# Moving two DMA issues, one matmul group, one vector add and four filler matmuls inside a four-engine pipeline

## The reference

```python
# second block, for each of 32 batches: attention with hyperbolic distances, 16 heads of 8
diff_sq = q_norm_sq + k_norm_sq - 2.0 * qk
denom = (1.0 - c * q_norm_sq) * (1.0 - c * k_norm_sq)
denom = jnp.maximum(denom, 1e-06)
cosh_arg = jnp.maximum(1.0 + 2.0 * c * diff_sq / denom, 1.0)
dist = jnp.arccosh(cosh_arg)
attn = softmax(-dist);  x = x + (attn @ v) @ wo.T
# then an MLP with 512 hidden units
x = x + jnp.einsum('bsw,wd->bsd', relu(layernorm(x) @ w1 + b1), w2) + b2
```

## Time and profile before

| what | value |
|---|---|
| median of 3 runs | 2447.98 us (2444.44 to 2456.33) |
| profiled execution, its own time | 2456.33 us |
| span of its trace | 2454.2 us |
| mean granted TensorE clock | 0.907 of full speed |
| busy over the span: PE, DVE, ACT, POOL | 85%, 80%, 72%, 66% |
| second block, first to last | about 1330 us to the end |

### The profile page before, as it was taken

How to read it: one execution, slowest core, us unless ns; L and a number is a source line. 1 busy time by engine, 2 the same in 40 slices (tenths; PEclk the granted TensorE clock), 3 DMA queues, 4 the chain that set the end, 5 groups by cost and what they waited for, 6 DMA issues and landing times. The chain is left out here.

```text
span 2454.2 us, 50808 instructions
## 1 busy us (share of the span) xinstructions
PE 2089.9 (85%) x15438; PEld 1566.8 (64%) x15438; DVE 1956.8 (80%) x5939; ACT 1767.4 (72%) x3085; POOL 1627.2 (66%) x1866
## 2 busy tenths in 40 slices
PE   4999999999999996999997677777777778777876
PEld 4677777777777775888885445555555555555554
DVE  4677776776777774778775899999999999999992
ACT  2666666666666762444432799999999999999996
POOL 2776676766666750000001899999999999999993
PEclk7999999999999996999997579888888988889888
DMA  5000000000000003353450466776666777666674
GB/s 142 1 2 2 2 1 2 2 1 2 1 2 1 2 2 70 86 119 76 96 114 10 93 127 130 139 138 128 124 119 127 141 141 134 119 129 124 129 142 80
DMA packets 81388, 184.24 MB, mean 75 GB/s; under 512 B 9479, under 2 KB 31530, under 8 KB 81195
## 3 DMA queue, kind: packets, MB, share of 16 engines
q0 software_dynamic: 36864, 134.23, 29.1%
q1 hardware_dynamic: 36010, 43.38, 7.9%
q10 hardware_dynamic: 8320, 4.19, 0.7%
HBM read 42.85 MB, written 4.72 MB: 19 GB/s over the span
## 5 line engine op out<-in xcount | busy, mean ns | idle before, releaser
L1557 POOL TENSOR_TENSOR spare<-spare,u 128x1024 f32<-128x1024 f32 x192 | 456.2, 2376 | 16.0
L542 ACT ACTIVATE prob<-s_ps,nmax 128x128 f32<-128x128 f32 (+1 forms) x1024 | 364.4, 432 | 132.2 <-DVE nmax L599 132.2
L599 DVE CUSTOM_DVE_ANT_0 s_ps<-s_ps,mask 128x128 f32<-128x128 f32 (+1 forms) x1024 | 340.7, 385 | 100.7 <-issue 76.4
L1633 DVE TENSOR_SCALAR u<-d_ps 128x1024 f32<-128x1024 f32 x256 | 312.1, 1219 | 48.7 <-PE i_ps L1374 48.1
L579 POOL TENSOR_TENSOR g_lo<-g_all,g_hi 128x512 fp32r<-128x512 f32 x256 | 329.1, 1286 | 21.4
L1637 DVE SCALAR_TENSOR_TENSOR u<-i_ps,u 128x1024 f32<-128x1024 f32 x256 | 313.5, 1225 | 13.2 <-DVE u L1633 0.5
L1374 PE MATMUL d_ps<-rowsT 28*128 28x256 f32 x1024 | 144.7, 357 | 149.5 <-DVE u L1637 145.9
L534 ACT COPY g_all<-g_ps 128x512 f32<-128x512 f32 x256 | 151.5, 592 | 162.6 <-PE g_ps L63 161.5
L1514 ACT ACTIVATE u<-u 128x1024 f32<-128x1024 f32 x256 | 257.0, 1056 | 1.7 <-DMA u<-spare 1.6
L1517 ACT ACTIVATE u<-u 128x1024 f32<-128x1024 f32 x256 | 255.7, 1051 | 0.0
L1374 PEld LDWEIGHTS d_ps<-rowsT 28*128 28x128 f32 x1024 | 92.4, 208 | 246.3 <-issue 241.7
(11 more groups left out here) (275 smaller groups left out, 5795.2 us busy)
## 6 DMA issues: line engine op xcount, KB each, us to landing
u<-spare POOLq DMA_DIRECT2D x256, 512.0 KB, 12.2
w_all<-w_rows SPq DMA_DIRECT2D x128, 256.0 KB, 5.9
x<-L_attn_x ACTq DMA_DIRECT2D x8, 512.0 KB, 13.9
y<-x SPq DMA_DIRECT2D x32, 128.0 KB, 10.0
wkqv<-L_attn_Wkqv SPq DMA_DIRECT2D x4, 528.0 KB, 8.9
gate_rows<-L_ffn_gate_proj SPq DMA_DIRECT2D x1, 512.0 KB, 14.4
up_rows<-L_ffn_up_proj SPq DMA_DIRECT2D x1, 512.0 KB, 11.1
down_cols<-L_ffn_down_proj SPq DMA_DIRECT2D x1, 512.0 KB, 13.0
```

What stands on the lines that cost most here:

```text
L542: last = nc.scalar.activation(prob[:, kind, at, :].rearrange("p c n -> p (c n)"), s_ps[kind][:, at.start * P:at.stop * P], ACT.Exp, bias=n ...
L599: last = nc.vector.tensor_tensor_reduce(out=scores, in0=scores, in1=keep.mask[:, N - width:N], scale=-1.0, scalar=3.4e38, op0=ALU.add, op1 ...
L1557: nc.gpsimd.tensor_tensor(extra, extra, pair, ALU.mult).then_inc(prod_done, 1)
L1633: nc.vector.tensor_scalar(u[:, slot(i, p), :], d_ps[:, :], 0.0, None, ALU.max).then_inc(dist_done, 1)
```

## The change

Five edits, all in the written orders of the second block:

1. POOL issues sums 0 and 1 behind product 4, ahead of product 5; sums 2 to 7 stay behind product 5.
2. The first half of the hidden layer moves from the end of p = 1 to p = 2, ahead of `pe_values`, so both halves stand at one place in the loop.
3. Filler matmuls in a batch go from 6 to 10: one is new ahead of the values at p = 3, six instead of four stand behind p = 4, two instead of one behind p = 7.
4. On DVE `dve_y` at p = 1 stands ahead of the copies of rows 5 and 6 instead of behind them.
5. The wait for a late copy, used in the last batch alone, moves with edit 2.

```diff
-    SUMS_BEHIND = {5: (0, 1, 2, 3, 4, 5, 6, 7)}
+    SUMS_BEHIND = {4: (0, 1), 5: (2, 3, 4, 5, 6, 7)}
-    HIDDEN_AT = (1, 3)
-    BUSY_AHEAD, BUSY_BEHIND = {5: 1}, {4: 4, 7: 1}
+    HIDDEN_AT = (2, 3)
+    BUSY_AHEAD, BUSY_BEHIND = {3: 1, 5: 1}, {4: 6, 7: 2}
...
-                        if four_before and p == HIDDEN_AT[1]:
-                            pe_hidden(pe, b - 4, 1, (b + 1) * (HP // 2))
+                        if four_before and p in HIDDEN_AT:
+                            if not one_after:
+                                pe.wait_ge(late_xT4_done, 1)
+                            pe_hidden(pe, b - 4, HIDDEN_AT.index(p), (b + 1) * (HP // 2))
                         if one_before and p in VALUES_AT:
                             pe_keep_busy(BUSY_AHEAD.get(p, 0))
...
-                        if four_before and p == HIDDEN_AT[0]:
-                            if not one_after:
-                                pe.wait_ge(late_xT4_done, 1)
-                            pe_hidden(pe, b - 4, 0, (b + 1) * (HP // 2))
...
+                        if p == 1 and five_before:
+                            dve_y(dve, b - 5)
                         for r in {0: (4,), 1: (5, 6), 2: (7,)}.get(p, ()):
                             copy_rows(dve, b, r, i)
-                        if p == 1 and five_before:
-                            dve_y(dve, b - 5)
```

## The result

The changed kernel is slower: 2568.57 us median of 4 runs (2557.45 to 2572.67) against 2447.4 us for the kernel before (four runs here), ratio 1.0489 (95% interval 1.0448 to 1.0531). The sign was forecast, the size was not: +121 us where I had +56.

A forecast was written before the change was run, and what follows sets the result against it. A loop through four engines, loop B at 34.94 us, was to bind; with 0.4 for slow stretches, 35.3 against 33.3 us over 27 batches gave 54 us, plus 2 at the end: 2504 us median, range 2470 to 2540.

The forecast's parts named there:

- The step that failed: TensorE: filler at p = 3 and moved hidden half cost nothing; 0.4 and 1.0 us if the waits covering them go.
- loop B: From mark over POOL's norm, PE's MLP output, DVE's residual and copies to next mark: 34.94 us, expected to bind.
- Loop A: ACT and POOL alone: sums 0 and 1 delay root 5 from 6.70 to 8.5 us; 33.87 us; rival chance 0.11.
- Loop B's leg over POOL's norm: POOL's product 5, four sums and norm end 14.12 us behind the mark, 2.39 later, so PE waits.
- The residual ahead of the copies: DVE at p = 1 waits for the MLP output before copying rows, so pair 2 starts 0.8 to 1.2 us later.
- Fillers: Two more behind p = 4 add 0.86 to 1.7 us; one behind p = 7 adds 0.43 to 0.85 at 1.2 GHz.
- clock collapse: PE's new waits at p = 0 lower the clock in nearly all batches: 36.9 us each, 2545 us; chance 0.14.

## Why the prediction missed

- **The step that failed** is the sentence that "the one at p = 3 and the moved hidden half fall into waits for DVE: nothing", with 1.0 as the price if the cover goes. The half did fall into such a wait (PE idles 1.30 us ahead of pair 4 in the kernel before). But I priced it by its length at its new place and never looked at its old one. It had stood ahead of PE's idle stretch at p = 1 and kept that short; the delay of pair 2, which I had worked out myself, made the rest longer. Gap 2.42 us, clock to 1.2 GHz, and three pieces of work at half speed between two pairs: 2.6 us of waiting a batch. Both ways of undoing it give back about that (66 and 62 us, 2.3 to 2.4 a batch).
- **Without that edit the number holds, and the path does not.** The prediction gave 35.3 us a batch and 2504 us; the kernel without the moved half gave 35.13 and 2502.3. But there PE waits for the norm in 4 batches only, 1.0 us in all, so loop B is not what binds it. The match is luck in good part.
- **Loop A** was nearly right up to root 5: it starts 8.35 us behind the mark against my 8.5, with ACT waiting 1.55 us. Product 5 took 3.97 us there, not the 4.26 I had taken from product 0. In the changed kernel the loop did not bind. Alone on the kernel before, the sums cost 33 us, not the 15 of loop A.
- **Loop B's leg over POOL's norm** binds in a third of the batches of the kernel with the sums alone, and in most batches of the changed kernel with the fillers as before (PE waits 16.1 us for the norm, 19 times). In the changed kernel PE waited only 1.8 us in all for the norm: that is done 13.47 us behind the mark, not 14.12 (the product, four sums and the norm were each a little shorter than my rows), and PE comes to its transpose at 14.14. There the residual starts 17.52 us behind the mark, against my 17.35, but by another way: late values, six fillers, pair 6 late by 1.26, two fillers at half clock behind p = 7, pair 1 late by 0.3. Two legs of like length; I had the one that was just covered.
- **The residual ahead of the copies**: forecast 0.8 to 1.2, shown as a wait of 1.1 to 1.4. Its price by itself was right (22 us alone). In the change it was worth 80, since it also opened the gap. I counted the delay as DVE's and did not ask what PE does meanwhile.
- **Fillers**: forecast 0.86 for pair 6, and 1.26 - 0.45 = 0.81 was found. The rule that I had set against it from the Trainium skill (TensorE: Matmul & The Clock Gate, "Why this matters for your kernels"), to leave TensorE no idle gaps, did not make these four fillers a gain (27 us lost with them alone). The traces agree with it at the gaps of p = 1 and p = 6, where filler gave back 62 and 17 us.
- **The rival "clock collapse"** (36.9 us a batch, 0.14) had the right kind and nearly the right size, and the wrong place: I put it at p = 7 and p = 0. The fillers behind p = 7 did run at half clock, but what that cost DVE at pair 1 is 0.3 us; the main part came at p = 2. The measured 37.34 lies above the 36.9, and 2568.57 us above my range.
- **Left open:** why the gap at p = 1 mostly gives a wait of 3.0 in the changed kernel and 1.68 with one to three edits less. The rows show how much of the stack runs at 1.2 GHz in each (all three pieces, or about two), not what fixes the moment at which the clock turns. It is not noise: the batch lengths repeat to about 0.02 us, in the changed kernel every three batches (37.69, 37.52, 37.42), with the moved half alone every six.

## What to carry to other kernels

A piece of work on TensorE, whose granted clock fell and stayed here with what it did before, has two prices: its length where it goes, and the gap where it came from; before moving it, read the idle time on both sides of its old place, with every delay the same change adds there. Put filler into the gap that stands just ahead of the slow stretch, and judge by granted clock and period, not by the number of fillers. And do not take the longest wait in the table for the bound: here it sat on POOL, and its 109 us moved with edits that never touched POOL.

## What the hardware showed that I had not expected

- The clock fell to 1.2 GHz around a gap of 2.42 us in which PE worked 0.21 of 2.60 us, and stayed at 1.00 when 2.33 of 2.50 us were filled. With the moved half alone, gaps of 1.76 us were followed by either clock.
- One useless matmul (0.60 us in the record) in a batch of 33 went with a granted clock of 0.97 instead of 0.89 from 1500 to 2300 us, and with less busy time of PE. Over whole executions the clock was 0.927 to 0.944 in its four runs, and 0.909 to 0.916 in those of the kernel before beside them.
- A kernel can settle into batches that are all a little slow: with the fillers alone nearly all last 34.0 to 34.2 us, each with the same two waits, while the kernel before mixes 32.4 and 34.0.
- On GpSimd the product right behind DMA issues took 4.26 us against 3.62. Product 5 behind two sums took 3.97 us in the changed kernel, and it stands in the chain of the kernel with the sums alone.
